# A fused FFN, attention, FFN block on one core: four low parts and three weight pieces of the first chunk change their place

## The reference, cut to what matters

```python
def reference(x, Wq, Wk, Wv, centroids, biases, Ws_up, Ws_down, W_up, W_down):   # x: 1 x 2048 x 128
    x = x + 0.5 * ffn(layernorm(x))
    x = x + attn(layernorm(x))          # softmax(q k^T) / sqrt(128) @ v
    x = x + 0.5 * ffn(layernorm(x))
    return x

def ffn(x):                             # 64 experts of hidden width 64, top 8 by biased affinity
    shared = silu(x @ Ws_up) @ Ws_down
    aff = x @ centroids.T
    idx = top_k(aff + biases, 8)
    w = sigmoid(aff[idx]); w = w / (sum(w) + 1e-8)      # cw: w at idx, zero elsewhere
    h = silu(einsum('td,edf->etf', x, W_up))
    y = einsum('etf,efd->etd', h, W_down)
    return shared + einsum('etd,te->td', y, cw)
```

## Time and profile before

| | |
|---|---|
| median of 3 runs | 581.1 us (579.74 to 582.62) |
| the profiled execution | 577.28 us, of which the span of the profile is 575.4 us |
| TensorE matmul busy | 547.6 us, 95% of the span |
| VectorE, ScalarE, GpSimd busy | 434.4, 408.3 and 278.2 us |
| mean granted TensorE clock | 0.993 of full speed |

### The profile page before, as it was taken

How to read it: one execution, slowest core, us unless ns; L and a number is a source line. 1 busy time by engine, 2 the same in 40 slices (tenths; PEclk the granted TensorE clock), 3 DMA queues, 4 the chain that set the end, 5 groups by cost and what they waited for, 6 DMA issues and landing times.

```text
span 575.4 us, 8712 instructions
## 1 busy us (share of the span) xinstructions
PE 547.6 (95%) x2737; PEld 442.6 (77%) x2737; DVE 434.4 (75%) x911; ACT 408.3 (71%) x808; POOL 278.2 (48%) x247
## 2 busy tenths in 40 slices
PE   7689999899989999899999999899999999999997
PEld 5466777677867778679999999778777777877885
DVE  6487679968996676577877978698768968875664
ACT  7667777687768777566666657576876787687774
POOL 3878765766676576200000000065674766566563
PEclk9799999999999999999999999999999999999999
DMA  8535564354545553000000000045554565566652
GB/s 274 159 119 172 165 195 157 126 173 166 169 135 179 179 166 127 0 1 2 1 1 2 0 2 1 1 139 176 173 185 153 169 189 158 168 172 193 186 186 101
DMA packets 44190, 72.22 MB, mean 126 GB/s; under 512 B 8848, under 2 KB 9552, under 8 KB 44144
## 3 DMA queue, kind: packets, MB, share of 16 engines
q1 hardware_dynamic: 43568, 71.17, 38.9%
q10 hardware_dynamic: 512, 0.36, 0.2%
q0 software_dynamic: 64, 0.13, 0.1%
HBM read 69.53 MB, written 2.10 MB: 124 GB/s over the span
## 4 chain that ended last, share of the span: by engine, by line
PE 76%; DVE 11%; POOL 5%; ACT 3%; issue 3%; DMA 0%; POOLq 0%; DVEq 0%; SPq 0%; ACTq 0%
PE lrow L965 11%; PE lrow L966 11%; PE lrow L967 11%; PE bank L1007 9%; PE bank L1009 8%; PE bank L1008 8%; PE bank L1013 5%; PE bank L1205 3%; PE bank L1207 3%; PE bank L1206 3%; POOL gpart_lo L252 2%; DVE rs L650 2%; DVE gated L625 1%; DVE rs L648 1%; PE bank L967 1%
## 5 line engine op out<-in xcount | busy, mean ns | idle before, releaser
L252 POOL TENSOR_TENSOR gpart_lo<-gated,gpart_hi 128x512 fp32r<-128x512 f32 x174 | 223.9, 1293 | 190.3 <-ACT gpart_hi L417 186.4
L406 ACT ACTIVATE lrow<-lrow 128x512 f32<-128x512 f32 (+1 forms) x252 | 147.3, 585 | 61.4 <-PE lrow L967 60.9
L625 DVE TENSOR_TENSOR gated<-lrow,wide 128x512 f32<-128x512 f32 x166 | 114.0, 687 | 47.2 <-ACT lrow L406 43.5
L417 ACT CAST gpart_hi<-gated 128x512 fp32r<-128x512 f32 x174 | 106.5, 613 | 7.5 <-DVE gated L625 6.8
L1007 PE MATMUL bank<-gpart_lo,wdn_hi 128*128 128x512 f32 x256 | 102.4, 400 | 6.5 <-POOL gpart_lo L252 6.3
L1009 PE MATMUL bank<-gpart_hi,wdn_hi 128*128 128x512 f32 x256 | 101.8, 398 | 0.0
L1008 PE MATMUL bank<-gpart_hi,wdn_lo 128*128 128x512 f32 x256 | 101.4, 396 | 0.0
L625 DVE TENSOR_TENSOR lrow<-lrow,wide 128x512 f32<-128x512 f32 x78 | 54.2, 694 | 29.8 <-ACT lrow L406 29.6
L417 ACT CAST gpart_hi<-lrow 128x512 fp32r<-128x512 f32 (+1 forms) x90 | 53.2, 591 | 31.0 <-DVE lrow L625 30.8
L1007 PEld LDWEIGHTS bank<-gpart_lo,wdn_hi 128*128 128x128 f32 x256 | 48.3, 189 | 21.3 <-issue 5.3
L252 DVE TENSOR_TENSOR gpart_lo<-lrow,gpart_hi 128x512 fp32r<-128x512 f32 (+1 forms) x90 | 61.4, 682 | 2.8 <-ACT gpart_hi L417 2.1
(11 more groups left out here) (209 smaller groups left out, 996.4 us busy)
## 6 DMA issues: line engine op xcount, KB each, us to landing
wide<-gates_dram SPq DMA_DIRECT2D x488, 128.0 KB, 3.0
raw<-in_w_up SPq DMA_DIRECT2D x8, 256.0 KB, 5.3
raw<-in_w_down SPq DMA_DIRECT2D x8, 256.0 KB, 5.5
gates_dram<-gates SPq DMA_DIRECT2D x8, 128.0 KB, 2.3
x<-in_x SPq DMA_DIRECT2D x3, 256.0 KB, 4.1
out_dram<-x SPq DMA_DIRECT2D x3, 256.0 KB, 3.0
x<-in_x SPq DMA_DIRECT2D x1, 128.0 KB, 2.3
x<-in_x ACTq DMA_DIRECT2D x1, 128.0 KB, 2.5
```

What stands on the lines that cost most here:

```text
L252: return eng.tensor_tensor(gpart[1][0:m, U % NGP, :], gated_at(U)[0:m, :], gpart[0][0:m, U % NGP, :].bitcast(F32), ALU.subtract)
L406: nc.scalar.activation(dst[0:m, :], hid[U % NH][0:m, :], ACT.Silu).then_inc(s_silu, 1)
L417: nc.scalar.copy(gpart[0][0:m, U % NGP, :], gated_at(U)[0:m, :]).then_inc(s_ghi, 1)
L625: nc.vector.tensor_tensor(gated_at(U), a, b, ALU.mult).then_inc(s_gated, 1)
```

## The change

`on_pool` now sends no unit up to 6 of the first pass to GpSimd: units 1, 2, 4 and 5 get their low part on VectorE (3 and 6 had it there already), and their gated values stay in PSUM. `PRE` falls from 6 to 3, so the pieces 3 to 15 are split in units 0 to 24 instead of pieces 6 to 15 in units 0 to 18. In ScalarE's stream the third piece goes ahead of the copies of the transposed weights, and within a unit the high part of the unit before now precedes the piece. The product of Wq and Wk is made after unit 18, its parts after 19 and 20.

```diff
-PRE = 6
+PRE = 3
@@ on_pool
-            return u % 3 != 0 and (u < UNITS - 1 or n % NCH < NCH - 1)
+            return u % 3 != 0 and (u < UNITS - 1 or n % NCH < NCH - 1) and (n > 0 or u > EARLY)
@@ ScalarE
                             silu_unit(2, n)
+                            piece_hi(2)
                             pro_cwT(n)
-                            piece_hi(2)
                             silu_unit(3, n)
-                            for k in range(3, PRE):
-                                piece_hi(k)
                     for u in range(UNITS):
                         if c or u >= LEADS[f]:
                             silu_unit(u, n)
+                        if c or u > 1 - f:
+                            hi_unit(*((u - 1, n) if u else (UNITS - 1, n - 1)))
                         if n == 0 and u % 2 == 0 and PRE + u // 2 < 2 * WP:
                             piece_hi(PRE + u // 2)
-                        if c or u > 1 - f:
-                            hi_unit(*((u - 1, n) if u else (UNITS - 1, n - 1)))
...
-                        if n == 0 and u == 16:
+                        if n == 0 and u == 19:
                             qk_hi()
@@ VectorE
-                        if n == 0 and u == 17:
+                        if n == 0 and u == 20:
                             qk_lo()
@@ TensorE
-                        if n == 0 and u == 15:
+                        if n == 0 and u == 18:
                             qk_weights()
```

## The result

| | before | changed |
|---|---|---|
| median (6 runs each) | 580.3 us (578.13 to 582.62) | 570.78 us (569.8 to 573.52) |
| ratio, 95% interval | | 0.9845 (0.9812 to 0.9878) |
| the profiled execution, its span | 577.28, 575.4 us | 572.29, 570.5 us |

The kernel is 1.55% faster, about 9.0 us; the forecast was 9.2, and 571.9 us. The first three runs of the kernel before had a median of 581.1 us, with three more it is 580.3.

What follows compares the result with a forecast made beforehand. The first pass up to `up(9)` was taken to hang on GpSimd's queue, not on TensorE. Terms 7.3 + 2.2 - 0.3 = 9.2 us against the median of 581.1 gave 571.9 us, range 568.5 to 577.0.

Steps and rivals of the forecast that it cites:

- the first part: First pass up to `up(9)`: it hangs on GpSimd's queue, not TensorE; the change brings 7.3 us, bounds 5.2 and 8.2.
- The walk through the new order: First pass to `up(9)`, new order with old durations: VectorE finds the root made at 22.45 us, `up(9)` starts at 26.9.
- The port: VectorE's root steps: an instruction working from SBUF alone waits for GpSimd's 1.25 us instruction; freed, the steps take 0.2 each.
- the first rival: Moved low parts held by the port, up to 1.29 us each instead of 0.68: gain 6.8, 574.3 us; chance 0.04.
- 2 us that are part of what follows: Ten matmuls of 23.93 to 28.3 us, 0.43 apart in place of 0.23: 2 us counted within the first part's gain.
- I take 2.4 GHz throughout: TensorE up to 25.0 us in the new order: longest gap some 0.5 us, so full clock assumed.
- the sign that the prediction gave: From 16 to 25 us: no TensorE idle time over 1 us and a granted clock of 1.00.
- The product's move: Product of Wq and Wk three units, 4.2 us, behind its inputs, so TensorE's wait of 1.36 us there goes.
- So the late low part that cost 0.86 us goes too: After `up(9)`: routing weights made between pieces 12 and 13, not after the last piece, so TensorE's 0.86 us wait goes.
- 2.2 less 0.3 forecast: `up(9)` to the end of the first pass: 2.2 us of waits removed, 0.3 us of new waits for GpSimd.
- GpSimd nearly without idle time: Sign of being right: GpSimd nearly without idle time from 28 to 55 us.
- The second rival: GpSimd becomes the bound after unit 9, instructions 1.35 apart, VectorE's chain still blocked: gain 5.4, 575.7 us; chance 0.22.

Runs made afterwards that it cites:

- experiments 2: Kernel before with only the changed `on_pool`: low parts of units 1, 2, 4, 5 on VectorE, six pieces ahead as before; 575.06 us, ratio 0.9918.
- 3: Changed kernel's new places of the pieces and ScalarE order, with low parts and the product of Wq and Wk as before; 576.46 us, ratio 0.9950 to the kernel before.
- 10: Kernel before with GpSimd's root for the second chunk right behind the six pieces, ahead of piece 6; 577.39 us, ratio 0.9973.
- 11: Changed kernel with one more piece in unit 5, where it meets VectorE's root steps; 572.61 us, ratio 0.9877 to the kernel before.
- 12: Kernel before with 18 unused matmuls into a free bank ahead of `down(1)`, to keep TensorE awake; 578.8 us, ratio 0.9988.
- experiment 4: Changed kernel with the product of Wq and Wk back after unit 15, its parts after 16 and 17; 571.25 us, ratio 0.9850 to the kernel before.
- experiment 6: Changed kernel with one more piece in unit 7, every later one two units sooner; 570.91 us, ratio 0.9857 to the kernel before.

## Why the prediction was right, and where it was not

The forecast was 571.9 us and the result 570.8, inside its range; the main mechanism was right, and the closeness of the number is in part luck.

- **What bounds the first part: right.** GpSimd's queue held it. The walk through the new order gave the root steps at 22.45 us (22.48 when the shift is taken off), piece 2 copied at 13.4 (13.4), and `up(9)` at 26.9; it came at 26.1 in one profile and at 26.3 in the other. The forecast's bounds were 26.0 and 29.0; the better one was nearly reached, because the root steps ran free and the first row tile, or both, got through. Term: 7.3, measured 7.9 to 8.1.
- **The port: right.** Neither part alone frees the steps (experiments 2, 3 and 10: two or three of three blocked), the whole does, and a piece put back among them blocks them again (11). The Trainium skill (SBUF — State Buffer, SBUF: two separate sides) calls it an exclusive lock for a whole instruction, which is what the ends at 24.07 and 24.05 us show. The four moved low parts, which read one operand from PSUM, took 0.68 to 0.69 us beside a busy GpSimd, so the first rival had nothing for it. Too wide was only the sentence that a VectorE instruction waits when it "works from SBUF alone": the pairs of BN_STATS took 0.47 us with GpSimd idle (14.86 us in the kernel before) and 0.48 beside a piece (17.13), and the reciprocal of the affinities, from SBUF to SBUF, took 1.74 us in all seven cases of the changed kernel, one of them beside a GpSimd low part (38.55 us).
- **"2 us that are part of what follows": wrong.** The low clock from 24 to 28 us cost nothing (12). The chain of waits there ran over GpSimd and VectorE, so slow matmuls of TensorE lay beside it. In experiment 3 a low clock of the same level cost 1.8 us: the next waits there (1.36 and 0.87 us) were as long as in the kernel before, so nothing took it up. The number 7.3 did not rest on it, since it was taken from end to end, but the sentence did. The 4.50 us of idle time weren't the loss either: they grew to 5.84 in experiment 10, and the kernel didn't get slower. "I take 2.4 GHz throughout" held in the second profile; in the first the clock was 0.50 from 18 to 20 us, against the sign that the prediction gave, and cost nothing either.
- **The product's move: right.** 1.36 us forecast, 1.31 in the profile of experiment 4, one profile against one; the medians can't tell it. In the kernel before VectorE's low part of Wq and Wk (46.71 us) stands straight behind the reciprocal of 1.75 us (45.05), and so it does in experiment 4 (39.36 behind 37.70): so the wait of 1.36 us was, by the order of VectorE's stream, one for that long instruction; no run tried to move it.
- **"So the late low part that cost 0.86 us goes too": wrong**, and with it the mis-sized term of the sum: 2.2 less 0.3 forecast, 0.5 measured. TensorE's waits from `up(9)` to the second transposes were 1.36 + 0.86 = 2.22 us before and 0.23 + 0.88 + 0.72 = 1.83 now, where 0.3 was forecast. I argued from where the products stand among the pieces. But what stands ahead of the low part of unit 19 is the same string as before. GpSimd of the changed kernel:

```profile
43.41 1.30 POOL L252 TENSOR_TENSOR gpart_lo<-gated,gpart_hi 128x512 fp32r<-128x512 f32 x1 [0.92 <-ACT gpart_hi L417]
44.66 1.48 POOL L339 TENSOR_TENSOR wdn_lo<-raw,wdn_hi 128x512 fp32r<-128x512 f32 x1
46.11 1.29 POOL L252 TENSOR_TENSOR gpart_lo<-gated,gpart_hi 128x512 fp32r<-128x512 f32 x1
47.36 1.30 POOL L339 TENSOR_TENSOR wup_lo<-raw,wup_hi 128x512 fp32r<-128x512 f32 x1
48.60 0.75 POOL L345 TENSOR_TENSOR rec<-rec,sil 128x256 f32<-128x256 f32 x1
49.43 0.74 POOL L346 TENSOR_TENSOR rec<-rec,rest 128x256 f32<-128x256 f32 x1
50.13 2.52 POOL L252 TENSOR_TENSOR gpart_lo<-gated,gpart_hi 128x512 fp32r<-128x512 f32 x2
```

  Low part of unit 16, piece, low part of 17, piece, two products, low part of 19: 6.72 us from 43.41 to 50.13, and before, with pieces 14 and 15 in place of 11 and 12, 6.72 us too (from 51.32 to 58.04, when its GpSimd had waited 2.16 us for the same high part).
- **"GpSimd nearly without idle time": wrong**, and a queue that waits for its inputs isn't helped by being shorter, which fits experiment 6. It waited 0.46, 0.40, 0.24 and 0.92 us for ScalarE's high parts between 31 and 44 us, 2.0 us in all. The last of them starts the string, and it goes back to VectorE:

```profile
38.55 1.74 DVE L686 RECIPROCAL rec<-aff_a 128x256 f32<-128x256 f32 x1
...
40.49 0.69 DVE L623 TENSOR_TENSOR lrow<-lrow,wide 128x512 f32<-128x512 f32 x1
```

  The reciprocal of the affinities, for the routing weights, holds the gating of unit 15 (the second row), ScalarE waits 0.55 us for it in order, the high part of unit 16 comes late, and the string begins. So it can explain 0.55 of the 0.92 us that GpSimd waited there. I had counted 23.4 us of GpSimd work from 27.8 to the transposes and got 51.2; it ended at 52.9 (54.49 less the shift). No run moved the reciprocal, so its part is argued from the order and the trace, not shown.
- **The rivals.** No new wait decided. The second rival had its mechanism in part (TensorE had new waits for GpSimd of 0.95 us in sum), but far from its price of 2 us plus blocked steps. The lower end of the range, 568.5, should be 568.7 by its own terms; nothing rests on it.

The forecast of 9.2 us was met by two errors of opposite sign: some 0.7 too little in the first part, 1.4 too much in the second. That they half cancel is luck. The first and second part together are 8.4 to 8.6 us in the profiles; the rest to 9.0 lies within the interval (7.1 to 10.9 us).

No version tried is faster than the change.

## What to carry to other kernels

Follow the wait back before pricing it: an idle time of 4.5 us with a low clock behind it was worth nothing by itself, since TensorE waited again right after, while a low clock behind 2.90 us cost 1.8 us where TensorE set the pace afterwards (experiment 3). And small instructions that the profile shows eight times too long, because they end only with the neighbour engine's instruction, stood for 3.2 us on VectorE's path. When work is moved out of a queue, look at what stands between the wait's own trigger and its end, not at the queue's total; if that string is unchanged, the wait will be there again. And compare profiles by distances between landmarks, since the arrival of the first loads and a clock that falls in some executions only move ends by as much as a term of the sum.

## What the runs showed of the hardware

- The granted clock fell in some executions and not in others at the same place of the same program: in the first profile of the changed kernel it was 0.50 from 18 to 20 us and 0.91 on the mean from 150 to 170, in the second 1.00 in both stretches, after waits of TensorE of the same length (1.76 us, and 1.4 us for the normalised rows). From 95 to 110 us it was 0.89 in the changed kernel and 1.00 in experiment 4, both after a wait of 1.36 us for the rows; it cost 1.05 us. I had taken executions to differ by their start alone.
- A float32 matmul of 256 columns shows as two instructions, together 0.44 us (36 instructions, 18 matmuls, in 7.93 us at a granted clock of 1.00).
- A low clock cost time here only where TensorE set the pace: nothing from 24 to 28 us of the kernel before, where a wait of 1.40 us for the rows followed and took it up, and 1.8 us from 30.66 us on in experiment 3, where the next wait stayed at its 1.36 us.
